# An mLSTM layer's score matmuls on two row tiles of 64 rows, with the PSUM banks shared out anew

## The reference

```python
qk = jnp.einsum('hsd,htd->hst', qh, kh) / np.sqrt(DH)
C = qk * D_mat
normalizer = jnp.maximum(jnp.abs(C.sum(axis=-1, keepdims=True)), jnp.exp(-max_log_D))
h = jnp.einsum('hst,htd->hsd', C / (normalizer + EPS), vh)
```

## Time and profile before

| | |
|---|---|
| median of three runs | 1262.59 us (1262.53 to 1263.86) |
| the profiled execution | 1252.59 us |
| its span, first to last instruction | 1250.8 us |
| granted TensorE clock, mean over the span | 0.784 of 2.4 GHz |
| busy: TensorE, VectorE, ScalarE, GpSimd | 1027.7, 719.0, 509.8, 506.3 us |
| mLSTM stage, arguments of the first tile to the last values | 107.8 to 243.2 us |

### The profile page before, as it was taken

The page is one execution under the profiler, slowest core; times in us unless marked ns, Lnnn a source line. Parts: engine busy times, 40 slices in busy tenths (PEclk is TensorE's granted clock), DMA queues, the critical chain, the costliest instruction groups (busy, mean ns, idle before and its releaser), DMA issues. The chain is left out here.

```text
span 1250.8 us, 26334 instructions
## 1 busy us (share of the span) xinstructions
PE 1027.7 (82%) x10017; PEld 736.9 (59%) x10017; DVE 719.0 (57%) x2205; ACT 509.8 (41%) x784; POOL 506.3 (40%) x566
## 2 busy tenths in 40 slices
PE   6715888675878848999992679989999989989998
PEld 1103666543555525666661567878888778856665
DVE  7662788875666654877773544444444546335554
ACT  2434777442333324666662223332233435222222
POOL 4200466666665651555556643444333441001110
PEclk9957999867787878999996555565555779669999
DMA  8324444151111122333321100111110211013331
GB/s 262 143 61 151 146 145 139 45 187 47 39 45 40 44 73 84 119 127 119 124 97 59 35 26 27 30 31 33 32 31 27 86 40 30 18 35 103 94 88 41
DMA packets 67628, 97.13 MB, mean 78 GB/s; under 512 B 18768, under 2 KB 40336, under 8 KB 66736
## 3 DMA queue, kind: packets, MB, share of 16 engines
q1 hardware_dynamic: 55376, 77.74, 19.9%
q0 software_dynamic: 8192, 16.79, 4.4%
q10 hardware_dynamic: 3936, 0.92, 0.4%
HBM read 64.75 MB, written 30.67 MB: 76 GB/s over the span
## 5 line engine op out<-in xcount | busy, mean ns | idle before, releaser
L1742 DVE TENSOR_REDUCE split_table<-attn_psN 128x16 f32<-128x1024 f32 x62 | 75.9, 1223 | 155.2 <-PE attn_psN L1539 151.2
L1539 PE MATMUL attn_psN<-attn_keys,attn_queries 32*128 32x128 f32 x992 | 136.0, 406 | 23.2 <-DMA early_ctxT<-in_ctxT 10.7
L1684 ACT ACTIVATE split_table<-attn_psT 128x2048 f32<-128x2048 f32 x32 | 60.1, 1877 | 196.9 <-PE attn_psT L1560 196.9
L1539 PEld LDWEIGHTS attn_psN<-attn_keys,attn_queries 32*128 32x128 f32 x992 | 105.8, 281 | 56.9 <-issue 35.8
L1006 POOL TENSOR_TENSOR moe_h_lo<-moe_hid,moe_h_hi 128x512 f16<-128x512 f32 x78 | 90.6, 1161 | 105.6 <-ACT moe_h_hi L1161 100.6
L1573 PEld LDWEIGHTS attn_psO<-heads_vheads,split_table 128*64 128x64 f32 x2048 | 100.3, 200 | 13.4 <-issue 8.8
L1573 PE MATMUL attn_psO<-heads_vheads,split_table 128*64 128x18 f32 x2048 | 107.1, 257 | 0.0
L1258 DVE SCALAR_TENSOR_TENSOR moe_hid<-moe_psU,split_to_hidden,moe_act_g 128x512 f32<-128x512 f32 x110 | 81.1, 748 | 41.2 <-ACT moe_act_g L1155 41.0
L1155 ACT ACTIVATE moe_act_g<-moe_psG,split_unscale 128x512 f32<-128x512 f32 x110 | 75.6, 687 | 59.1 <-PE moe_psU L1090 43.9
L1556 PE MATMUL attn_psT<-attn_queries,attn_keys 32*128 32x128 f32 x1024 | 90.3, 433 | 4.3 <-DVE attn_shift L1758 3.6
L1556 PEld LDWEIGHTS attn_psT<-attn_queries,attn_keys 32*128 32x128 f32 x1024 | 78.1, 291 | 9.1 <-DVE attn_shift L1758 7.0
(11 more groups left out here) (263 smaller groups left out, 2592.7 us busy)
## 6 DMA issues: line engine op xcount, KB each, us to landing
mlstm_vals<-in_values SPq DMA_DIRECT2D x16, 544.0 KB, 3.4
mlstm_keys<-in_keys SPq DMA_DIRECT2D x16, 512.0 KB, 3.4
scratch_ys<-cell_h SPq DMA_DIRECT2D x26, 256.0 KB, 2.0
res_x<-in_x SPq DMA_DIRECT2D x16, 256.0 KB, 6.3
early_ctxT<-in_ctxT SPq DMA_DIRECT2D x16, 256.0 KB, 6.3
scratch_x<-split_table SPq DMA_DIRECT2D x16, 256.0 KB, 2.3
ffn_x<-scratch_x SPq DMA_DIRECT2D x32, 128.0 KB, 2.9
out<-raw_keys SPq DMA_DIRECT2D x32, 128.0 KB, 2.3
```

Source lines behind the costliest of these rows:

```text
L1539: ins = pe.matmul(bank[:, at:at + P], queries[g % 3][rows, b, :, :].rearrange("p n t -> p (n t)"), keys[g % 3][rows, b, :, :].rearrange("p ...
L1684: act.activation(probT[half][:, :, :, :].rearrange("p r b q -> p (r b q)"), psT[:, :], ACT.Exp).then_inc(prob_done, 1)
L1742: v.tensor_reduce(peak[:, :, 2 * i:2 * i + 2, :], plain_bank(g, i).rearrange("p (r b m t) -> p r b m t", r=HR, b=2, m=HM), AX.X, ALU.max). ...
```

## The change

Scores go on two row tiles of 64 rows. Rows 0 to 63 hold pairs 0 and 1, rows 64 to 127 pairs 2 and 3. Two masked copies of the queries are enough: copy m keeps pair m of each half. Each sequence takes two f32 matmuls of 128 columns, one for each half of the rows, written to two different banks. `psS` has four banks (two for each of two tiles), `psA` one, and three banks of values rotate. So arguments of tile n wait for the exponential of tile n-1, and the third and fourth values of a group (from group 1 on) also for the division of the group before. Score columns are now in the order half, sequence, pair in half; the decay operands, the `m_rows` stores (twelve DMAs instead of six, with the same bytes) and the columns that values read follow it. ScalarE makes two copies of a group's queries instead of four.

```diff
@@ phase_decay, sync
                 for c in range(2):
-                    sp.dma_start(s["m_rows"][2 * n + c].rearrange("(b m t) -> b m t", m=HP0, t=S),
-                                 m_parts[:, n, :].rearrange("b (m h t) -> b m h t", m=HP0, h=2)[:, :, c, :]).then_inc(m_stored, 16)
-            sp.wait_ge(m_stored, ONE + 16 * 2 * NSPLIT)
+                    rows = s["m_rows"][2 * n + c].rearrange("(i r b m t) -> b i r m t", r=2, b=2, m=HP0 // 2, t=S)
+                    for b2 in range(2):
+                        sp.dma_start(rows[b2], m_parts[b2::2, n, :].rearrange("b (r m h t) -> b r m h t", r=2, m=HP0 // 2, h=2)[:, :, :, c, :]).then_inc(
+                            m_stored, 16)
+            sp.wait_ge(m_stored, ONE + 16 * 4 * NSPLIT)
@@ phase_mlstm
+    HR, HM = 2, 2
+    RH = D // HR
-        qmask = r.sb("qmask", [D, HP0])
+        qmask = r.sb("qmask", [D, HM])
-        queries = [r.sb(f"queries{k}", [D, GB, HP0, S]) for k in range(2)]
+        queries = [r.sb(f"queries{k}", [D, GB, HM, S]) for k in range(2)]
-        psA = [r.ps(f"psA{k}", [P, N]) for k in range(2)]
-        psS = [r.ps(f"psS{k}", [P, N]) for k in range(2)]
-        psV = [[r.ps(f"psV{k}{i}", [P, 512]) for i in range(2)] for k in range(2)]
+        psA = r.ps("psA", [P, N])
+        psS = [r.ps(f"psS{k}", [P, HR * 512]) for k in range(2)]
+        psV = [r.ps(f"psV{k}", [P, 512]) for k in range(3)]
+        def values_bank(g, half):
+
+            return psV[(2 * g + half) % 3]
@@ tensor
-                if n_ >= 2:
-                    pe.wait_ge(decay_done, ONE + n_ - 1)
-                pe.matmul(psA[c][:, :], dk[g % 2][:, i * P:(i + 1) * P], dq[g % 2][:, i, :], start=True, stop=True).then_inc(arg_done, 1)
+                if n_:
+                    pe.wait_ge(decay_done, ONE + n_)
+                pe.matmul(psA[:, :], dk[g % 2][:, i * P:(i + 1) * P], dq[g % 2][:, i, :], start=True, stop=True).then_inc(arg_done, 1)
                 for b2 in range(2):
                     b = 2 * i + b2
-                    ins = pe.matmul(psS[c][:, b2 * HP0 * S:(b2 + 1) * HP0 * S], keys[g % 2][:, b, :, :].rearrange("p n t -> p (n t)"),
-                                    queries[g % 2][:, b, :, :].rearrange("p m t -> p (m t)"), start=True, stop=True)
+                    for rr in range(HR):
+                        rows, at = slice(rr * RH, (rr + 1) * RH), rr * 512 + b2 * HM * S
+                        ins = pe.matmul(psS[c][:, at:at + HM * S], keys[g % 2][rows, b, :, :].rearrange("p n t -> p (n t)"),
+                                        queries[g % 2][rows, b, :, :].rearrange("p m t -> p (m t)"), start=True, stop=True)
@@ values
-                if g >= 2:
-                    pe.wait_ge(h_done, ONE + g - 1)
+                if g >= 2 or g and i >= 2:
+                    pe.wait_ge(h_done, ONE + (g if i >= 2 else g - 1))
-                        at, col = (i % 2) * H0 * VW0 + 2 * m * VW0, (b2 * HP0 + m) * S
+                        at, col = (i % 2) * H0 * VW0 + 2 * m * VW0, (m // HM * 2 * HM + b2 * HM + m % HM) * S
@@ scalar
-            spread_queries(0, (0, 1, 2, 3))
+            spread_queries(0, (0, 1))
-                    spread_queries(g + 1, (0, 1))
+                    spread_queries(g + 1, (0,))
-                    spread_queries(g + 1, (2, 3))
+                    spread_queries(g + 1, (1,))
@@ vector
-                v.scalar_tensor_tensor(out=cT[c][:, :], in0=psS[c][:, :], scalar=float(DH0) ** -0.5,
-                                       in1=decay[c][:, :], op0=ALU.mult, op1=ALU.mult).then_inc(cT_done, 1)
+                by_rows = lambda t: t[:, :].rearrange("p (r n) -> p r n", r=HR)
+                v.scalar_tensor_tensor(out=by_rows(cT[c]), in0=by_rows(psS[c])[:, :, 0:2 * HM * S], scalar=float(DH0) ** -0.5,
+                                       in1=by_rows(decay[c]), op0=ALU.mult, op1=ALU.mult).then_inc(cT_done, 1)
@@ layouts
-    pair_of = np.repeat(np.arange(2 * HP0), S)
+    pair_of = np.repeat([b2 * HP0 + m for half in range(2) for b2 in range(2) for m in (2 * half, 2 * half + 1)], S)
-        "qmask0": (np.arange(D)[:, None] // DH0 // 2 == np.arange(HP0)[None]).astype(np.float32),
+        "qmask0": (np.arange(D)[:, None] // DH0 // 2 % 2 == np.arange(2)[None]).astype(np.float32),
```

More of the change, by code:

```diff
@@ L670, in values @@
                     pe.wait_ge(vals_in[g % 2], ONE + 16 * (g // 2 + 1))
-                if g >= 2:
-                    pe.wait_ge(h_done, ONE + g - 1)
+                if g >= 2 or g and i >= 2:
+                    pe.wait_ge(h_done, ONE + (g if i >= 2 else g - 1))
                 for m in range(HP0):
                     for b2 in range(2):
-                        at, col = (i % 2) * H0 * VW0 + 2 * m * VW0, (b2 * HP0 + m) * S
-                        ins = pe.matmul(psV[g % 2][i // 2][b2 * S:(b2 + 1) * S, at:at + 2 * VW0], cT[c][:, col:col + S],
+                        at, col = (i % 2) * H0 * VW0 + 2 * m * VW0, (m // HM * 2 * HM + b2 * HM + m % HM) * S
+                        ins = pe.matmul(values_bank(g, i // 2)[b2 * S:(b2 + 1) * S, at:at + 2 * VW0], cT[c][:, col:col + S],
                                         vals[g % 2][:, (2 * i + b2) * HP0 + m, :, :].rearrange("p n w -> p (n w)"), start=True, stop=True)
@@ L702, in spread_queries @@
                                          ACT.Identity, scale=qmask[:, m:m + 1])
-                if part[-1] == HP0 - 1:
+                if part[-1] == HM - 1:
                     ins.then_inc(queries_done, 1)
@@ L710, in decays @@
                     act.wait_ge(cT_done, ONE + n_ - 1)
-                act.activation(decay[c][:, :], psA[c][:, :], ACT.Exp).then_inc(decay_done, 1)
+                act.activation(decay[c][:, :], psA[:, :], ACT.Exp).then_inc(decay_done, 1)
             act.wait_ge(const_in, ONE + 16 * 6)
-            spread_queries(0, (0, 1, 2, 3))
+            spread_queries(0, (0, 1))
             for g in range(GROUPS):
@@ L744, in divide @@
                 v.wait_ge(values_done, ONE + TILES * (g + 1))
-                flat = [psV[k][i][:, 0:2 * H0 * VW0].rearrange("p (h w) -> p h w", w=VW0) for i in range(2)]
+                flat = [values_bank(g, i)[:, 0:2 * H0 * VW0].rearrange("p (h w) -> p h w", w=VW0) for i in range(2)]
                 halves = [slice(2 * i, 2 * i + 2) for i in range(2)]
-                sums = [psV[k][i][:, 0:2 * H0 * VW0].rearrange("p (t h w) -> p t h w", t=2, h=H0)[:, :, :, DH0] for i in range(2)]
+                sums = [values_bank(g, i)[:, 0:2 * H0 * VW0].rearrange("p (t h w) -> p t h w", t=2, h=H0)[:, :, :, DH0] for i in range(2)]
                 least = [early.floor[:, g * TILES + 2 * i:g * TILES + 2 * i + 2, :] for i in range(2)]
```

## The result

The changed kernel takes 1309.33 us (median of 4 runs, 1295.87 to 1321.3); the kernel before, run beside it, 1263.22 us (median of 4, 1262.53 to 1273.72). The ratio is 1.0309, with a 95% interval of 1.0208 to 1.0411: slower, by 39 us on 1262.6 when the ratio is taken at its word. The profiled execution of after took 1321.3 us, the slowest of its four, so its stages are compared one by one, and its total is not taken as the size of the change.

A forecast was written before the change was run, and what follows sets the result against it. TensorE and VectorE take turns in the mLSTM loop; at 1.2 GHz TensorE alone bounds it: +38.0 us, less 2 for clock returns, other edits zero, so 1262.6 + 36 = 1298.6 us. Range 1274 to 1308, rival 2 (alternating clock) included.

The forecast's parts named there:

- the share of the array in use: mLSTM stage: inferred to decide the clock instead of busy time; counted columns fall from 3104 to 2080 a tile.
- The clock: mLSTM stage: largest term; starts at 1.2 GHz and stays there with half-height scores, +38.0 us before returns, +36 after.
- 840 to 980 us of the attention: Stretch of the kernel before, TensorE busy 136.81 of 140 us yet granted 0.50; cited as evidence for the low clock.
- The tile at 1.2 GHz: mLSTM stage: arguments 0.54, scores 1.16, values 1.01, sum 2.71 us a tile, with TensorE alone the bound.
- rival 3: mLSTM scores: row tiles do not run in pairs; 3.47 us a tile, +87 us, 1350; chance 0.05.
- The term for returns to 1.00: mLSTM stage: a return or two to the high clock, estimated to take 2 us off the +38.0.
- The tile at 2.4 GHz: mLSTM stage: loads wait 0.32 us behind arguments, eight score streams take 0.71; group 7.76 us, 0.46 less.
- rival 1: Whole mLSTM stage: clock holds at 2.4 GHz, so faster; -6.9 us, 1255.7; chance 0.07.
- Its condition: mLSTM stage: clock must rise at its start and not be dropped by the pause of 1.56 us a group.
- Banks, stores, query copies, two-bank weighing at nothing: mLSTM stage and decay-row stores: the other edits cost zero; stores covered by 4 us, weighing at most 0.1 us a tile, hidden.
- later stages as long as before: Stages after the mLSTM stage: expected unchanged in length, as a sign that the forecast is right.
- the scale: Whole kernel: profile 1252.59 against median 1262.59 us, 10 us apart; difference added to the median; 2.5 us tells from no change.

The follow-up runs named there:

- e2: Changed kernel plus 13 whole-height matmuls of 512 columns before the first group, to start the stage at full clock; 1311.01 us (4 runs).
- e5: Changed kernel with score loops exchanged: both sequences on rows 0 to 63 first, then rows 64 to 127; 1295.89 us, ratio 1.0292.
- e9: Changed kernel run and profiled again without any edit; 1312.43 us (6 runs), ratio 1.0379 to the kernel before.
- e3: Changed kernel plus three whole-height matmuls of 238 columns before each group's third values; 1273.82 us, ratio 1.0131 to the kernel before.
- e8: e7 with the added matmuls in the pauses of groups 0 to 7 alone; 1275.4 us (2 runs).
- e7: e4 with 15 matmuls in front instead of 13, and five before the first values of groups 13 and 14; 1271.38 us (6 runs).
- e1: Kernel before with only the new PSUM sharing, one arguments bank and three rotating value banks; 1271.19 us, ratio 1.0093.
- e4: Changed kernel with both 13 whole-height matmuls before the first tile and three in each group; 1271.25 us, ratio 1.0022.

## Why the prediction was right, and what it missed

The direction was right, and so was what made it: the clock stays at 1.2 GHz and a tile then takes 2.7 us. The reason given for the clock, the share of the array in use, fits the runs and is not shown alone. The forecast of 1298.6 us was 10.7 us low, and 1309.33 is 1.3 us above the range. Taken by the ratio instead, 1.0309 times 1262.59 is 1301.6, 3 us above the forecast.

- **The clock**: forecast to stay at 1.2 GHz through the stage. It was 0.50 in after, e2, e5 and e9. That busy time does not decide was inferred from the attention; e3 and e8 show it for this stage, and show that whole-height work beside the row tiles can lift and hold the clock. That it is the share of the array is an inference still: 840 to 980 us of the attention, on which the prediction rests, also holds the four-tile scores that lift the clock elsewhere. In the kernel before the clock does not rise at once, as the prediction says, but 3.1 us after the stage starts. The Trainium skill (TensorE: Matmul & The Clock Gate, "Why this matters for your kernels") has TensorE stay at the high clock if it is kept busy with short pauses between bursts. Here it was busy for 172.71 of 172.90 us and stayed at 0.50; for this stage the measurement decides against that rule. What was not tried is filling the pause with part-height matmuls, half-height streams without any 64-column values, or whole-height scores in eight streams of 128 columns. So how height, width and the open load weigh against each other stays open.
- **The tile at 1.2 GHz**: 0.54 + 1.16 + 1.01 = 2.71; measured 0.54 + 1.16 + 1.00 = 2.70. Two row tiles run at a time, so rival 3 falls.
- **The term for returns to 1.00, 2 us off**: there were none; the stage took 172.7 us where 64 x 2.71 = 173.4 less 2 was forecast. The term is +37.3, not +36.
- **The tile at 2.4 GHz**, seen in e7 and e8: the scores start 0.32 us behind the arguments and take 0.71, both as forecast from the attention's rows; the tile takes 1.56 us, the group 7.81 where 7.76 was forecast, and the pause 1.51 where 1.56 was. The "up to twice" of the Trainium skill (TensorEngine Tiling (Array Packing), "Theoretical Speedup") gives, as an estimate, 0.52 for the scores. The trace does not reach it: 1.03 to 0.71 is 1.45 times, and with the load that is no longer hidden 1.25 to 1.03 is 1.2 times.
- **The price of rival 1**: -6.9 us over the stage, 0.46 a group; e7 has 0.41 a group and 5.4 over the stage. Its condition did not come by itself: the clock falls at the pause of 1.5 us a group (e8) and the start at 1.2 GHz is not left (after).
- **Banks, stores, query copies, two-bank weighing at nothing**: e1 has 0.6 us for the banks; the stores end 6.4 us ahead of their cover; the query copies and the two-bank weighing have no run of their own, but TensorE waits for no exponential.
- **What failed**: "later stages as long as before", and with it the scale. I took one offset of 10 us between the profile and the runs and rounded the range out for it; nor are the 2.5 us right that it gives as what a measurement can tell from no change. The kernel before alone spreads over 39 us in 23 runs. In the profiles much of it is the attention's clock: the same attention takes 473.8 us in after, 459.2 in e9 and 443.4 in e5. The medians differ by 46.1 us, the ratio says 39, the stage 37.3: the excess over the stage is of the size of that spread. Over all runs here the fastest of before is 1249.93 and of the changed kernel 1294.31, 44 apart; the slowest are 1288.89 and 1321.3, 32 apart. 37 lies between the two. Whether the change also makes high spells of the attention rarer, by a few us, these runs cannot tell.

## What to carry to other kernels

Before cutting a matmul into row or column tiles, look at the granted clock of stages that already run such tiles: a TensorE that is busy all the time at 0.50 is a warning that they may not lift it; it is no proof, since other stretches of the same attention rose on row tiles. Work out the change at both levels of the clock; here the same edit is -5 us at one and +37 at the other. What picks the level is not busy time; that it is how much of the array works is the reading that fits. And take more than three runs of a kernel with stages that sit between the levels before trusting a scale to 10 us.

## What was not expected of the hardware

- Three useless whole-height matmuls a group (2.75 us at 1.2 GHz, 1.47 at 2.4) made the changed stage faster by 25 us, 172.7 to 147.7; with 15 in front of the stage and five in each of two groups besides, by 43, to 130.0 (e7).
- At 1.2 GHz, with no pause at all, the changed stage did not rise once in 172 us, in two profiles; the kernel before, after its one drop, was back in 3.4 us. The same kernel's attention rose behind 3.3 us of 32-row tiles alone (708.2 to 711.5 us).
- Added whole-height matmuls lift the clock only at times: of six rounds that began at 1.2 GHz (e3 and e4), it rose in or right behind three (116.93 and 252.53 in e3, 234.54 in e4) and not at the other three.
- Streams start in pairs also when the program gives all of one half first (1.23 us in e5, as in after); that the two of a pair lie on different halves is not seen.
- The same attention code took 443 to 474 us in eleven profiles, with a mean clock of 0.54 to 0.60.
